# Expert groups turned ahead of the outputs in front, and b1 carried in the rows of w1

## The reference

```python
x = x + 0.5 * _L0_ffn_ref(_layernorm(x), ...)
x = x + _L0_attn_ref(_layernorm(x), ...)
x = x + 0.5 * _L0_ffn_ref(_layernorm(x), ...)
x = x + 0.5 * _L1_ffn_ref(_layernorm(x), ...)
x = x + _L1_attn_ref(_layernorm(x), ...)
x = x + 0.5 * _L1_ffn_ref(_layernorm(x), ...)
```

```python
logits = x_flat @ Wr + br
topk_w, topk_idx = jax.lax.top_k(softmax(logits), 2)
topk_w = topk_w / sum(topk_w)
h = einsum('nc,ech->neh', x_flat, W1) + b1
h = (h - mean(h)) * rsqrt(var(h) + 1e-5) * g1 + be1
h = gelu(h, approximate=False)
expert_out = einsum('neh,eho->neo', h, W2) + b2
y = sum over the two chosen experts of expert_out * topk_w
```

## Time and profile before

| | |
|---|---|
| median of three runs | 627.59 us (627.01 to 629.43) |
| the profiled execution | 628.28 us, of which its span in the trace is 626.1 |
| mean granted TensorE clock | 0.896 |
| busy, share of the span | TensorE 82% (its weight loads 43%), VectorE 77%, ScalarE 52%, GpSimd 23% |
| m3 | about 339 to 409 us |
| m5 | 526 to 626 us, with the last gathers and additions |

### The profile page before, as it was taken

How to read it: one execution, slowest core, us unless ns; L and a number is a source line. 1 busy time by engine, 2 the same in 40 slices (tenths; PEclk the granted TensorE clock), 3 DMA queues, 4 the chain that set the end, 5 groups by cost and what they waited for, 6 DMA issues and landing times.

```text
span 626.1 us, 9476 instructions
## 1 busy us (share of the span) xinstructions
PE 512.6 (82%) x3033; PEld 270.7 (43%) x3033; DVE 484.3 (77%) x1373; ACT 327.0 (52%) x645; POOL 142.0 (23%) x188
## 2 busy tenths in 40 slices
PE   7687979989999999899585899877797786899800
PEld 3452322322223222244252777665555454777600
DVE  6997989898888998686987666897888758666722
ACT  2345546866676676798132688744242102678700
POOL 3000020000000000000075703654000072713645
PEclk9776969999999999999786899998797878899955
DMA  5006400028815000000225295421000015273432
GB/s 202 1 1 157 91 1 1 18 67 152 248 65 136 3 1 2 1 3 2 76 106 157 87 276 154 122 64 34 2 2 1 0 58 152 70 215 85 132 95 67
DMA packets 55981, 48.62 MB, mean 78 GB/s; under 512 B 5758, under 2 KB 48190, under 8 KB 55678
## 3 DMA queue, kind: packets, MB, share of 16 engines
q1 hardware_dynamic: 35326, 31.31, 18.4%
q0 software_dynamic: 4224, 8.59, 4.8%
q10 hardware_dynamic: 16384, 8.13, 4.5%
HBM read 24.94 MB, written 20.60 MB: 73 GB/s over the span
## 4 chain that ended last, share of the span: by engine, by line
PE 49%; DVE 25%; issue 9%; POOL 7%; ACT 4%; DMA 4%; SPq 1%; POOLq 0%; ACTq 0%; DVEq 0%
PE ps L747 7%; PE ps L716 7%; PE ps L737 7%; POOL rows_in L1105 5%; DVE arena L803 4%; PE ps L1193 4%; PE ps L1216 4%; POOL arena L1130 2%; PE ps L1555 2%; PE ps L1174 2%; PE ps L1201 2%; DVE stat L249 1%; ACT arena L1687 1%; PE ps L1499 1%; PE ps L545 1%
## 5 line engine op out<-in xcount | busy, mean ns | idle before, releaser
L803 DVE TENSOR_REDUCE arena<-ps 128x1 f32<-128x512 f32 x256 | 162.2, 682 | 25.4 <-PE ps L716 25.0
L869 ACT ACTIVATE arena<-ps 128x512 f32<-128x512 f32 x256 | 138.3, 603 | 58.5 <-PE ps L737 57.1
L716 PE MATMUL ps<-arena 96*128 96x512 bf16 x256 | 98.4, 397 | 7.9 <-DVE arena L803 6.8
L737 PE MATMUL ps<-arena 99*128 99x512 bf16 x256 | 96.4, 388 | 3.3 <-DMA arena<-arena 2.7
L1105 POOL DMA_INDIRECT rows_in<-xl,route x64 | 62.6, 978 | 149.9 <-DVE route L1061 131.6
L1130 POOL DMA_INDIRECT arena<-rows_out,route x64 | 61.3, 957 | 78.9 <-DMA rows_out<-arena 52.2
L747 PE MATMUL ps<-arena 128*32 128x512 f32 x512 | 68.2, 605 | 0.6 <-ACT arena L869 0.4
L737 PEld LDWEIGHTS ps<-arena 99*128 99x128 bf16 x256 | 24.9, 99 | 73.9 <-ACT arena L869 48.9
L716 PEld LDWEIGHTS ps<-arena 96*128 96x128 bf16 x256 | 25.1, 99 | 51.7 <-DVE arena L803 34.5
L1280 ACT ACTIVATE arena<-ps,route 128x128 f32<-128x128 f32 x124 | 46.4, 460 | 1.3 <-PE ps L1201 1.2
L1327 DVE TENSOR_REDUCE arena<-arena 128x4 f32<-128x512 f32 (+1 forms) x32 | 21.2, 663 | 30.4 <-ACT arena L1270 30.3
(11 more groups left out here) (283 smaller groups left out, 853.8 us busy)
## 6 DMA issues: line engine op xcount, KB each, us to landing
arena<-rows_in SPq DMA_DIRECT2D x28, 256.0 KB, 5.3
rows_out<-arena ACTq DMA_DIRECT2D x28, 256.0 KB, 2.5
rows_in<-zerob SPq DMA_DIRECT2D x2, 1920.0 KB, 11.2
arena<-att_parts SPq DMA_DIRECT2D x12, 256.0 KB, 8.7
arena<-in_consts SPq DMA_DIRECT2D x2, 1024.0 KB, 5.8
arena<-zerob SPq DMA_DIRECT2D x1, 2048.0 KB, 12.0
arena<-att_parts SPq DMA_DIRECT2D x14, 128.0 KB, 8.2
att_parts<-arena SPq DMA_DIRECT2D x6, 256.0 KB
```

The source lines that it names most:

```text
L716: pe.matmul(ps[:, bank, :], a_qs[0:96, b, h, j * P:(j + 1) * P], a_ks[0:96, b, h, keys * 512:(keys + 1) * 512], start=True, stop=True).the ...
L737: pe.matmul(ps[:, score_bank(n), :], a_ks[0:99, b, h0 + h4, i * P:(i + 1) * P], a_qs[0:99, b, h0 + h4, half * 512:(half + 1) * 512], start ...
L803: nc.vector.tensor_reduce(a_nm[:, k % 2, o % 2, k // 2:k // 2 + 1], ps[:, bank, :], AX.X, ALU.max, negate=True).then_inc(a.mpu, 1)
L869: nc.scalar.activation(a_p[:, n % 16, :], ps[:, score_bank(n), :], ACT.Exp, scale=0.25).then_inc(a.ex, 1)
```

## The change

It does four things.

1. **The order in the groups' loops.** Both engines' loops now run over all groups but the last. TensorE does `turn(u)`, then `out(u - 1)`, then the rows and hidden layer that `ahead` names: of group 3 in iteration 0, of groups 4 and 5 in iteration 1, of u + 4 from then on. ScalarE does `gelu(u)`, `store(u - 2)`, `out_in(u - 1)`, and then the rows and squares of the same groups.
2. **Half of the output copies go to VectorE.** `BY_VECTOR` gives it every odd group and the last four. `out_in(v - 4)` stands behind the first sum of a pair; the last four stand behind the last scaling, ahead of `behind()`. The semaphore `t.yc` is parted in two, and `wait_out_in` waits for the right one.
3. **b1 has no product any more.** A row's features sum to zero. So with d = b1 - w1[0] added to every one of the 128 rows of an expert's w1, and one added to the row's first feature, the product is x @ w1 + w1[0] + d = x @ w1 + b1. SP loads b1 and w1's row 0 broadcast over the partitions (two loads of 1 MB) once four of the attention's octets are done, between its own transfers of octets 5 and 6; GpSimd subtracts in eight steps between its own octets 6 and 7; VectorE adds to w1 in `centre_experts`, where b1's means and parts go. The `pick` product of L1191 goes, and so does b1's half of `brow` and of the gathers.
4. **The one is added to `xl` in `moe_vector_slots`**, as a step of its own with a yield, behind the statement that sets `m.base`. The callers' numbers of steps are as before.

```diff
-        brow = sb("brow", [24, B, 4, 2, P], BF16)
+        brow = sb("brow", [24, B, 4, P], BF16)
...
+        r_b1, r_w10 = arena_f(16384, NE, P), arena_f(0, NE, P)
...
+        BY_VECTOR = [g % 2 == 1 or g >= 2 * NGR - 4 for g in range(2 * NGR)]
+        FREED = 1
+
+        def wait_out_in(eng, u):
+
+            done = (BY_VECTOR * (u // (2 * NGR)) + BY_VECTOR)[:u + 1]
+            if BY_VECTOR[u % (2 * NGR)]:
+                eng.wait_ge(t.yc_v, done.count(True))
+            else:
+                eng.wait_ge(t.yc_a, done.count(False))
+
+        def moe_pool_b1(pool):
+
+            pool.wait_ge(s_b1w, 32)
+            for i in range(8):
+                pool.wait_ge(a.mpu, turn_at[NO - 2] + 3 * i)
+                two = slice(2 * i, 2 * i + 2)
+                ins = nc.gpsimd.tensor_tensor(r_b1[:, two], r_b1[:, two], r_w10[:, two], ALU.subtract)
+            ins.then_inc(s_b1, 1)
 
...
+            dve.wait_ge(m.n.xl_a, m.n.applied[b] + 1)
+            dve.wait_ge(m.n.xl_v, m.n.applied[b] + 1)
+            first = xl[:, TB * b:TB * (b + 1), 0]
+            yield vs.mark(nc.vector.tensor_scalar(first, first, 1.0, None, ALU.add))
             dve.wait_ge(m.base, m.i + 1)
             u = r_u.rearrange("p (e t) -> p e t", e=NE)
...
         def moe_scalar_store(act, m, g):
             b, u = m.b, NGR * m.i + g
-            act.wait_ge(t.yc, u + 1)
+            wait_out_in(act, u)
             k = tiles_in(g)
...
                 bank = HIDDEN_BANKS[u % 4]
-                pe.matmul(ps[:, bank, :], pick[:, g, :], brow[:, m.b, :, 0, :], start=True, stop=False)
                 for j in range(k):
                     ins = pe.matmul(ps[:, bank, j * P:(j + 1) * P], t_xt[:, u % 2, j * P:(j + 1) * P],
-                                    w1[:, :, :].rearrange("c e f -> c (e f)")[:, bass.ds(at[j], P)], start=False, stop=(j == k - 1))
+                                    w1[:, :, :].rearrange("c e f -> c (e f)")[:, bass.ds(at[j], P)], start=True, stop=True)
                 ins.then_inc(t.h, 1)
 
...
             def turn(u):
                 g = (u - u0) % NGR
                 pe.wait_ge(t.z, u + 1)
+                if u > u0:
+                    pe.wait_ge(t.ac, u if last - u > 3 else u - 1)
                 for j in range(tiles_in(g)):
...
+                if g == 0:
+                    pe.wait_ge(m.brow, 48 * m.turn)
                 bank = out_bank(last - u)
-                if u == last - 1:
-                    pe.wait_ge(t.yc, u - 1)
-                elif u >= u0 + 1 and u != last - 2:
-                    pe.wait_ge(t.yc, u)
+                if u > u0 and last - u != 3:
+                    wait_out_in(pe, u - 1 if last - u > 2 else u - 2)
                 regs, at = where.pop(u)
-                pe.matmul(ps[:, bank, :], pick[:, g, :], brow[:, m.b, :, 1, :], start=True, stop=False)
+                pe.matmul(ps[:, bank, :], pick[:, g, :], brow[:, m.b, :, :], start=True, stop=False)
...
                 hidden(u)
                 between(u - u0)
             routed(pair[1])
-            for u in range(u0, last - LEAD):
+            for u in range(u0, last):
                 turn(u)
-                if u + LEAD + 1 < last:
-                    turn_in(u + LEAD + 1)
-                hidden(u + LEAD)
-                out(u)
-            turn(last - 3)
-            turn(last - 2)
-            out(last - 3)
-            turn(last - 1)
-            out(last - 2)
+                if u > u0:
+                    out(u - 1)
+                for v in ahead(u - u0):
+                    if v + 1 < 2 * NGR:
+                        turn_in(u0 + v + 1)
+                    hidden(u0 + v)
             out(last - 1)
 
+        def ahead(g):
+
+            first = g + LEAD + (1 if g > FREED else 0)
+            return range(first, min(g + LEAD + (1 if g >= FREED else 0), 2 * NGR - 1) + 1)
+
         def turn_bank(left):
 
-            return TURN_IN_BANKS[0] if left == 2 else TURN_BANK
+            return TURN_IN_BANKS[0] if left in (1, 3) else TURN_BANK
 
...
-            for u in range(u0, last - LEAD):
+            for u in range(u0, last):
                 gelu(u)
-                if u > u0:
-                    store(u - 1)
-                if u + LEAD + 1 < last:
-                    rows(u + LEAD + 1)
-                squares(u + LEAD)
-                out_in(u)
-            gelu(last - 3)
-            store(last - 4)
-            gelu(last - 2)
-            out_in(last - 3)
-            gelu(last - 1)
-            store(last - 3)
-            out_in(last - 2)
+                if u > u0 + 1:
+                    store(u - 2)
+                if u > u0 and not BY_VECTOR[u - 1 - u0]:
+                    out_in(u - 1)
+                for v in ahead(u - u0):
+                    if v + 1 < 2 * NGR:
+                        rows(u0 + v + 1)
+                    squares(u0 + v)
             store(last - 2)
-            out_in(last - 1)
             store(last - 1)
 
...
+            def out_in(u):
+                k = tiles_in(u)
+                dve.wait_ge(t.y, u + 1)
+                if u >= 4:
+                    dve.wait_ge(t.ys[u % 4], 16 * (u // 4))
+                nc.vector.tensor_copy(t_y[:, u % 4, 0:k, :], ps[:, out_bank(last + 1 - u), 0:P * k].rearrange("p (j f) -> p j f", f=P))\
+                    .then_inc(t.yc_v, 1)
...
                 for v in groups:
                     summed(v)
+                    if v == groups[0] and v >= u0 + 5:
+                        out_in(v - 4)
                 dve.wait_ge(t.sqr, groups[-1] + 1)
                 vs.finish(Chain(rstds(groups[0], groups[-1])))
                 for v in groups:
                     scaled(v)
+            for v in range(last - 3, last + 1):
+                out_in(v)
             behind()
 
...
-            sp.wait_ge(s_b1, 2)
-            for i, parts in enumerate((b1p, b2p)):
-                sp.dma_start(bias_parts[:, i], parts[:, :, :]).then_inc(s_b1row, 16)
+            att_sync_negmax_rows(sp, 5, 6)
+            sp.wait_ge(a.done, 4)
+            sp.dma_start(r_b1, A["b1"].rearrange("(o e) f -> o e f", o=1).to_broadcast([P, NE, P])).then_inc(s_b1w, 16)
+            sp.dma_start(r_w10, A["w1"][:, 0:1, :].rearrange("e o f -> o e f").to_broadcast([P, NE, P])).then_inc(s_b1w, 16)
+            att_sync_negmax_rows(sp, 6, NO)
+            sp.wait_ge(s_b2, 1)
+            sp.dma_start(bias_parts, b2p[:, :, :]).then_inc(s_b2row, 16)
...
             pool.wait_ge(s_set, 10)
-            att_pool_negmax(pool, steps, range(1, NO))
+            att_pool_negmax(pool, steps, range(1, NO - 1))
+            moe_pool_b1(pool)
+            att_pool_negmax(pool, steps, range(NO - 1, NO))
             moe_pool_send(pool, m3[0])
             moe_pool_send(pool, m3[1])
...
-            dve.wait_ge(s_mix, 64)
-            mw, mb = small[:, 20, 0:NE], small[0:NE, 21, 0:1]
+
+            dve.wait_ge(s_mix, 48)
+            dve.wait_ge(s_b1, 1)
+            mw = small[:, 20, 0:NE]
+            vs.step(nc.vector.tensor_tensor(w1[:, :, :], w1[:, :, :], r_b1, ALU.add))
             vs.step(nc.vector.tensor_reduce(mw, w1[:, :, :], AX.X, ALU.add))
             vs.step(nc.vector.tensor_scalar(mw, mw, 1.0 / P, None, ALU.mult))
             vs.step(nc.vector.tensor_tensor(w1[:, :, :], w1[:, :, :], bc(mw.unsqueeze(2), [P, NE, P]), ALU.subtract))
-            vs.step(nc.vector.tensor_reduce(mb, b1[:, :], AX.X, ALU.add))
-            vs.step(nc.vector.tensor_scalar(mb, mb, 1.0 / P, None, ALU.mult))
-            vs.step(nc.vector.tensor_scalar(b1[:, :], b1[:, :], mb, None, ALU.subtract))
```

More of the change, by code:

```diff
@@ L98, in build @@
         n_rows = (2 * S // P + NE - 1) * P
-        bias_parts = nc.dram_tensor("bias_parts", [NE, 2, 3, P], BF16, kind="Internal").ap()
+        bias_parts = nc.dram_tensor("bias_parts", [NE, 3, P], BF16, kind="Internal").ap()
         rows_in = [nc.dram_tensor(f"rows_in{b}", [n_rows, P], F32, kind="Internal").ap() for b in range(B)]
@@ L1112, in moe_pool_bias @@
             pool.wait_ge(m.tix, m.i + 1)
-            pool.wait_ge(s_b1row, 32)
+            pool.wait_ge(s_b2row, 16)
             if m.i:
                 pool.wait_ge(Moe.rows_got[1 - m.b], 48 * ((m.i - 1) // B + 1))
-            pool.indirect_dma_start(out=r_bias[0:32].rearrange("p w i f -> p (w i f)"), out_offset=None,
-                                    in_=bias_parts.rearrange("e w i f -> e (w i f)"),
+            pool.indirect_dma_start(out=r_bias[0:32].rearrange("p i f -> p (i f)"), out_offset=None,
+                                    in_=bias_parts.rearrange("e i f -> e (i f)"),
                                     in_offset=bass.IndirectOffsetOnAxis(ap=r_tix[m.b][0:32], axis=0)).then_inc(m.bias, 16)
@@ L1181, in hidden @@
                     pe.wait_ge(m.tab, m.i + 1)
-                    pe.wait_ge(m.brow, 48 * m.turn)
                 regs = [pe.alloc_register(f"e{u}_{j}") for j in range(4)]
@@ L1233, in moe_tensor @@
             routed(pair[1])
-            for u in range(u0, last - LEAD):
```

(20 more changed lines are left out.)

24 lines of the change are left out of this document (7 added, 17 removed).

## The result

The changed kernel took 633.67 us (median of 9 runs, 631.67 to 638.51), the kernel before beside it 629.43 us: ratio 1.0084, 95% interval 1.0054 to 1.0114. A second measurement, further down, gave 634.23 us against 629.0, ratio 1.0066 (1.0037 to 1.0094). Slower by 4 to 5 us, where 633.0 us and +5.4 were forecast.

What follows compares the result with a forecast made beforehand. TensorE's chain bounds the expert stages, GpSimd's sends the way into m3. Late cast 5.15, m3's loop +1.3, its end -0.8, m5 -0.2: +5.4 us, 633.0 us for the median; range 628.8 to 636.5.

Steps and rivals of the forecast that it cites:

- The late cast: Slots of m3's first half: the added step puts the cast behind seven large operations, first send +5.15 us.
- w1's preparation: VectorE's extra pass over w1 and GpSimd's eight subtractions fit in idle time: 0, at most 5 us.
- m3's loop: First expert stage, from its start to the first gathers: 47.4 us against 46.1 before, so +1.3 us.
- Rival B: Expert loops: b1's bf16 product ahead of f32 weights is worth up to 0.61 us, not 0.32; 627.2 us; chance 0.08.
- m3's end: End of the first expert stage: the chain of sixteen gathers now leads, -0.8 us.
- The linear stage: Between m3 and m5: nothing waits for anything not shifted, so m5 starts 5.65 us later.
- m5: Second expert stage: -1.8 us, plus 1.6 for half clock behind a 3 to 4 us wait for group 8's rows: -0.2.
- A: Late cast but a clean run: first send 0.96 us, no clock costs in m3's ramp or m5; 629.0 us; chance 0.22.
- D: Slots of m3's first half: the cast stays where it was, +0.15 for 5.15; about 628 us; chance 0.04.
- C: Expert loops: VectorE sets the period, 0.33 us per group from the added copy, +6; 639 us; chance 0.06.

Runs made afterwards that it cites:

- the early cast: Changed kernel with the caller advancing the slots five steps instead of four ahead of the copy of xt: 630.15 us, ratio to the kernel before 1.0013.

## Why the prediction was right

**The late cast** was the largest term, +5.15 us, and it measured 5.16. The first send took 1.21 us instead of the 1.87 that I kept, but the fourth and fifth sends took 1.36 and 1.14 us, so the transposes came at +5.11 all the same. The experiment that takes this term alone out of the changed kernel gives 4.1 us of the 5.2 back. That the two differ lies within the intervals.

**w1's preparation** cost nothing, as it said. GpSimd's eight subtractions took 0.73 us each (forecast 0.65), VectorE's L428 behind the preparation starts at 282.32 where it was 282.31, after an idle time of 0.57 instead of 1.09, and the norm ahead of the slots at 308.51 instead of 308.50.

**m3's loop** was right in its sum, +1.1 against +1.3, by errors that cancel. The step that failed is the one that priced b1's product: "In the earlier trace rows it takes 0.32 us of TensorE's chain, so a group takes 3.38 us." It measured 3.18, and by my own words a period under 3.2 would have made me wrong. Rival B had the right mechanism, a bf16 product ahead of f32 weights, with 0.61 us as its bound; I put 0.08 on it because the chain had no gap. A gap of the loader isn't a gap in that chain, since the product behind it is counted as longer. From group 8's rows to the end of the hidden layer ahead of group 7's store there are five such groups, 5 x 0.20 = 1.0 us won. What took it back stands in the timeline of the changed kernel (second profile):

```profile
366.68 0.65 PE L1223 MATMUL ps<-cst,arena 128*128 128x128 f32 x4 [0.37 <-DVE arena L1372]
...
368.56 0.37 PE L1236 MATMUL ps<-brow,pick 24*128 24x512 bf16 x1 [1.22 <-DVE arena L1352]
...
370.63 1.06 PE L1196 MATMUL ps<-cst,arena 128*128 128x128 f32 x4
```

The output of group 2 waits for VectorE's copy of group 1, which stands behind the first sum of a pair, and 1.22 us go. The four transposes of group 8 then take 1.06 us instead of 0.60, at the lower clock. So TensorE came to group 8 at +26.3 instead of +25.5 (0.8), and its rows with the hidden layer beside them took 2.1 us instead of 1.3 (0.8). I had the low clock as "up to 1.6" and took none of the wait. Last, the first gather started 3.3 us behind that last hidden layer (391.63 - 388.31), where the prediction has 0.6 + 3.6 = 4.2 (0.9 won). That is -1.0 + 0.8 + 0.8 - 0.9 = -0.3 from rounded terms, and -0.2 measured. So the agreement of this term is luck.

**m3's end** was -0.62 against -0.8: the gathers lead, and VectorE's last copy ends ahead of the last gather, as it said. (By the earlier trace rows the way from L1346's end to L249 is 4.78 us, not 4.85; nothing hangs on it.)

**The linear stage** was the second step that failed: "Nothing in that stage waits for anything not shifted". Nothing did, but it started at half the clock. Its products wait behind m3's end, where TensorE now stands idle for two stretches of 3.10 and 2.27 us ahead of the transposes of x; the kernel before has 0.58 and 0.37 there. The stage took 1.15 us more in the second profile, 1.83 in the first, where I had 0. The rows show 2.35 us lost by the first product with bvs (5.80 against 3.45); that the 1.15 at the stage's end are what is left of them is argued, and no run tests it. I had priced that clock in m3 and in m5 and forgotten it at the one place where the change lengthens the wait on TensorE without adding a wait of its own: the gathers lead by more, because TensorE is done earlier.

**m5** was -0.17 against -0.2: all that is won ahead of group 8's rows is lost in the wait for them (3.81 us), as forecast. Its -0.2 came by two errors that cancel. From group 8's rows to the last gathers it took 44.69 us against 45.69, 1.0 less, where 1.9 won and 1.6 lost to the half clock would be 0.3 less: part of the 0.20 us per group that I missed. And group 8's rows were there 30.31 us behind m5's first transposes instead of 29.48, 0.8 later where I had 0.14. The second half's first send accounts for under 0.1 of that (4.35 us behind the same transposes, before 4.29); what delayed the rows behind it, no run shows.

Sum of the second profile: 5.11 + 1.14 - 0.62 + 1.15 - 0.17 = 6.6 us, where the prediction has 5.4. The span grew by 6.7, and the medians by 4.2 and 5.2. In the first profile, with its 1.45 us of delay at the norm taken off, the same terms are 5.12, 0.76, -0.72, 1.83 and -0.34: one execution's small terms are known to some 0.7 us. So the forecast's total was nearer than its terms deserved. And its 633.0 was counted from a kernel before of 627.59 us, which took 629.43 beside the changed one; that 633.67 lies so close to 633.0 is in part this difference.

Of the rivals, A had the shorter first send right (1.21 us, not quite its 0.96), but the clock costs that it took out were there. D didn't come, since the cast did move; with the early cast, where it stays, the kernel takes 630.15 us. C didn't come: no rows show VectorE holding the loop behind its first groups.

## What to carry to other kernels

- Where a caller counts a generator's steps, a new `yield` moves everything behind it. Compare the order of the instructions on that engine before and after, and see which one another engine waits for.
- Read the price of a product from the period with and without it, or look at the weight loader too. Here a bf16 product between f32 ones cost 0.52 us and not its own 0.32, because the next f32 weights came later.
- Work that is taken away may have been a cover. Here b1's product hid gelu in the old order, and TensorE's later end had kept the clock at 1.00 into the next stage.

## What the hardware showed that I had not expected

- A bf16 product of 24 rows by 512 columns ahead of f32 products costs 0.32 us and 0.20 more at the products behind it (1.09 against 0.89), whether they add to its result or overwrite it.
- Around two waits of 3.10 and 2.27 us on TensorE with 1.09 us of work between them the granted clock was 0.50 for some 13 us (it fell in the first one), and 16 f32 products of 128x16 took 3.60 instead of 1.96 us. Products of zeros in the waits kept it at 1.00.
- On three of the four chips that the experiments ran on, every kernel took 711 to 735 us, and all the waits that the profile calls `remote` ended within one of GpSimd's rows of 16 or 17 indirect DMAs or up to 3.3 us behind it, wherever in the execution that was. On the fourth chip the same DMAs came without such waits. What makes a chip one kind or the other isn't settled.
